# One graph-network kernel: the edge sums in 35 chunks a step and 45 half-width products instead of 36 chunks and 36 full-width products

## The reference

```python
xn = _layernorm(x)
msgs = edge_val[:, None] * xn[edge_src]                      # 212500 rows of 256
agg = jax.ops.segment_sum(msgs, edge_dst, num_segments=N)    # edge_dst is sorted
support = (1.0 + eps) * xn + agg
h = jax.nn.relu(support @ W1.T + b1)
x = x + (h @ W2.T + b2) + _L0_mix_ref(xn[None], ...)[0]
x = x + _L0_ffn_ref(_layernorm(x)[None], ...)[0]             # top-k routing, gelu, two products
```

## Time and profile before

| what | value |
|---|---|
| median of 3 runs | 2581.78 us |
| the profiled execution's own time | 2585.47 us |
| its span, first to last instruction | 2583.9 us |
| mean granted TensorE clock | 0.986 |
| TensorE busy | 2472.5 us, 96% |
| TensorE weight loads busy | 2151.3 us, 83% |
| GpSimd busy | 1712.5 us, 66% |
| VectorE busy | 1794.8 us, 69% |
| ScalarE busy | 1430.8 us, 55% |

### The profile page before, as it was taken

One profiled execution on the slowest core, in us unless ns is written; L12 is line 12 of the kernel. 1 busy time (PEld: TensorE's weight loads), 2 busy tenths in 40 slices (PEclk: granted clock), 3 DMA queues, 4 the chain that ended last, 5 costly groups with the idle time before them and its releaser, 6 DMA issues.

```text
span 2583.9 us, 41907 instructions
## 1 busy us (share of the span) xinstructions
PE 2472.5 (96%) x12655; PEld 2151.3 (83%) x12655; DVE 1794.8 (69%) x5939; ACT 1430.8 (55%) x3219; POOL 1712.5 (66%) x1881
## 2 busy tenths in 40 slices
PE   4789999999999999999999999999999999999996
PEld 4777888888888888888888888888888888888786
DVE  8847776776767768677677676776867767767567
ACT  3545665656656556466565664655646656556431
POOL 1247777777777777777777777777777777777400
PEclk9889999999999999999999999999999999999998
DMA  6734444344443444443434444344444343443338
GB/s 206 256 110 123 121 122 127 115 118 127 119 130 112 119 119 118 128 121 117 121 114 119 127 118 130 112 118 120 118 126 123 115 125 113 118 127 118 89 118 283
DMA packets 192003, 333.42 MB, mean 129 GB/s; under 512 B 46286, under 2 KB 133964, under 8 KB 191672
## 3 DMA queue, kind: packets, MB, share of 16 engines
q0 software_dynamic: 86752, 238.17, 31.6%
q1 hardware_dynamic: 105018, 92.42, 11.2%
HBM read 291.99 MB, written 38.46 MB: 128 GB/s over the span
## 4 chain that ended last, share of the span: by engine, by line
PE 86%; DVE 8%; DMA 3%; ACT 2%; issue 1%; SPq 0%; DVEq 0%
PE bank L1170 26%; PE qkv L1265 13%; PE bank L1277 13%; PE bank L1184 10%; PE bank L1214 6%; PE qkv L1194 5%; PE bank L1239 3%; PE bank L1230 3%; PE qkv L1193 2%; PE bank L1204 2%; DMA work<-in_x 2%; DVE rings L975 1%; DMA xn_dram<-work 1%; DVE work L422 1%; DVE work L393 1%; PE bank L1251 1%
## 5 line engine op out<-in xcount | busy, mean ns | idle before, releaser
L781 POOL DMA_INDIRECT rings<-xn_dram,window x1764 | 1686.7, 956 | 643.7 <-issue 377.2
L1170 PE MATMUL bank<-rings 128*128 128x256 f32 x3528 | 884.6, 380 | 16.1 <-DVE rings L975 13.2
L1170 PEld LDWEIGHTS bank<-rings 128*128 128x128 f32 x3528 | 653.8, 190 | 105.3 <-DVE rings L975 22.1
L975 DVE TENSOR_SCALAR rings<-iota,window_dst,window 128x128 f32<-128x128 f32 x1764 | 560.1, 358 | 160.8 <-PE bank L1170 138.8
L1265 PE MATMUL qkv<-work,ffn_weights 128*128 128x256 f32 x1568 | 365.5, 381 | 0.0
L1277 PE MATMUL bank<-ffn_weights,work 128*128 128x256 f32 x1568 | 362.0, 379 | 0.0
L871 ACT ACTIVATE work<-qkv,fb 128x256 f32<-128x256 f32 x392 | 160.1, 473 | 312.5 <-PE qkv L1265 312.0
L1277 PEld LDWEIGHTS bank<-ffn_weights,work 128*128 128x128 f32 x1568 | 297.2, 190 | 40.0
L1265 PEld LDWEIGHTS qkv<-work,ffn_weights 128*128 128x128 f32 x1568 | 295.7, 191 | 38.6
L1184 PE MATMUL bank<-resident,weights 128*128 128x256 f32 x1176 | 280.5, 382 | 0.0
L853 ACT ACTIVATE work<-bank 128x512 f32<-128x512 f32 x49 | 29.3, 597 | 403.2 <-PE bank L1222 403.2
(11 more groups left out here) (241 smaller groups left out, 3241.6 us busy)
## 6 DMA issues: line engine op xcount, KB each, us to landing
rings<-xn_dram,window POOLq DMA_INDIRECT x1764, 2.8
xn_dram<-work SPq DMA_DIRECT2D x14, 896.0 KB, 8.3
work<-xn_dram SPq DMA_DIRECT2D x49, 256.0 KB, 2.8
work<-in_x SPq DMA_DIRECT2D x48, 256.0 KB
out<-work SPq DMA_DIRECT2D x48, 256.0 KB
work<-in_x SPq DMA_DIRECT2D x7, 896.0 KB, 7.7
rings<-in_x SPq DMA_DIRECT2D x6, 896.0 KB, 9.4
rings<-out SPq DMA_DIRECT2D x6, 896.0 KB, 8.4
```

Source lines behind the costliest of these rows:

```text
L781: nc.gpsimd.indirect_dma_start(out=msg[q][:, :], out_offset=None, in_=xn_dram[:, :], in_offset=bass.IndirectOffsetOnAxis(ap=window[t % WIN ...
L975: v.tensor_scalar(sel[k % SEL_RING], iota[:, :], window_dst[b][:, k % SLOTS:k % SLOTS + 1], window[b][:, k % SLOTS, 2:3].bitcast(F32), ALU ...
L1170: te.matmul(agg[h], sel[k % SEL_RING], msg[q], start=first, stop=last, skip_group_check=True).then_inc(slot_used, 1)
```

## The change

The two accumulators of 128 nodes become four of 64: `agg[h][side * 64:(side + 1) * 64]`. A selection matrix has 64 columns, and a product writes 64 partitions of the accumulator, from partition 0 (side 0) or 64 (side 1). A step takes 35 chunks from the exact first edge of the *step*. Quarter q of the step's 256 nodes is multiplied with the chunks QUARTERS[q], which overlap at the borders: 10 + 12 + 12 + 11 = 45 products. Each chunk is gathered once; ten of them are used by two quarters. `products()` orders them so that sides alternate. If a quarter's edges lie outside its chunks, extra chunks are taken, whose number `tables_extra` works out on VectorE from the bounds (for any input; a second DMA of `dst` shifted by one edge tests whether `dst` is sorted).

Other edits: SEL_RING 12 to 22 (of half size), LEAD 8 to 12, two windows of a whole step instead of four of a tile, loaded in seven DMAs (one per block of chunks), `remainder` once a step, the orders PE_AT and DVE_AT, fewer end-of-row semaphores in the last stage, one reduction less and one compare and reduction more (`tables_order`) in the first part. GpSimd's second gather now stands behind a wait for `extra_stored` and two register loads.

```diff
-SEL_RING = 12
-LEAD = 8
+SEL_RING = 22
+LEAD = 12
 EARLY_EDGES = 12
-WINDOWS = 4
+WINDOWS = 2
+SLOTS = 35
+BLOCKS = (0, 7, 10, 15, 19, 24, 27, 35)
+QUARTERS = ((0, 10), (7, 19), (15, 27), (24, 35))
+LEFT = ((0, 1, 2, 3, 4, 5, 6, 7, 8, 9), (15, 16, 17, 18, 19, 20, 21, 22, 23, 24, 25, 26))
+RIGHT = ((10, 11, 12, 13, 14, 7, 8, 9, 15, 16, 17, 18), (27, 28, 29, 30, 31, 32, 33, 34, 24, 25, 26))
...
+def products():
+    order = []
+    for h in range(2):
+        for left, right in itertools.zip_longest(LEFT[h], RIGHT[h]):
+            order += [(2 * h + side, k) for side, k in enumerate((left, right)) if k is not None]
+    return order
...
         def tables_rows(pool):
+            pool.dma_start(rows_next[:, :, :].bitcast(I32), dst[1:ROWS + 1].rearrange("(c p j) -> p c j", p=P, j=P)
+                           ).then_inc(next_landed, 16)
...
+        def tables_order(dve):
+            v = nc.vector
+            dve.wait_ge(next_landed, 16)
+            v.tensor_tensor(rows, rows, rows_next.bitcast(I32), ALU.is_gt).then_inc(order_compared, 1)
+            dve.wait_ge(order_compared, 1)
+            v.tensor_reduce(unsorted_col, rows.rearrange("p c j -> p (c j)"), AX_X, ALU.max).then_inc(order_ready, 1)
...
+            tables_extra(dve)
...
-        PE_AT = dict(sup=0, x3=0, qkv=10, w1=1, h1=(12, 17, 20), w2=4, outT=(13, 23), ft=(16, 27), hid=(23, 23,
-                     27, 29), y=(31, 32, 32, 35))
+        PE_AT = dict(w1=5, w2=11, qkv=18, outT=22, ft=26, h1=30, late=34, hid=38, y=41)
...
+            for i in range(NS):
+                pool.wait_ge(window_landed[i % WINDOWS], WINDOW_DONE * (i // WINDOWS + 1))
+                for n, k in enumerate(GATHERS):
...
+                        pool.wait_ge(slot_used, RING + back * STEP_PRODUCTS + FREED[m] + 1)
...
+                    if n == 0:
+                        if i == 0:
+                            pool.wait_ge(extra_stored, 16)
+                        more = [pool.value_load(extra_count[0:1, 2 * i + h:2 * i + h + 1], min_val=0, max_val=ET)
+                                for h in range(2)]
...
+                v.tensor_scalar(sel[at_ % SEL_RING], iota[:, q * H:(q + 1) * H], window_dst[b][:, k:k + 1],
+                                window[b][:, k, 2:3].bitcast(F32), ALU.is_equal, ALU.mult).then_inc(sel_ready, 1)
...
-                te.matmul(agg[h], sel[k % SEL_RING], msg[q], start=first, stop=last,
-                          skip_group_check=True).then_inc(slot_used, 1)
+                te.matmul(agg[h][side * H:(side + 1) * H], sel[(i * STEP_PRODUCTS + n) % SEL_RING], msg[gathered % RING],
+                          start=first, stop=n == STEP_PRODUCTS - 1, skip_group_check=True).then_inc(slot_used, 1)
...
+                edges_to(PE_AT["w1"])
+                if j >= 0:
+                    tail_w1(j)
+                edges_to(PE_AT["w2"])
```

More of the change, by code:

```diff
@@ new lines, in rem_chunk @@
+                g.indirect_dma_start(out=rem_msg[:, :], out_offset=None, in_=xn_dram[:, :],
+                                     in_offset=bass.IndirectOffsetOnAxis(ap=rem_edges[:, 0:1], axis=0)
+                                     ).then_inc(rem_landed, 16)
+                for side in range(2):
+                    g.tensor_scalar(inside[:, side:side + 1], chunk, float(QUARTERS[2 * h + side][0]), BIG,
+                                    ALU.is_ge, ALU.mult)
+                g.tensor_scalar(dst_col, rem_edges[:, 1:2], float(-2 * P * i), None, ALU.add).then_inc(rem_dst_ready, 1)
@@ L1068, in step @@
                 last = i == NS - 1
[L1069 removed]
+                for k in range(STEP_PRODUCTS):
+                    if k == DVE_AT["stage"] and not last:
+                        start_step(i + 1)
                     ahead = k + LEAD
[L1071 removed]
+                    nxt = ahead >= STEP_PRODUCTS
                     if not (last and nxt) and not (i == 0 and ahead < EARLY_EDGES):
[L1073 to L1077 removed]
+                        edge(i + nxt, ahead % STEP_PRODUCTS)
                     if j >= 0:
@@ new lines, in step @@
+                if j >= 0:
+                    tail_w2(j, ran(i))
+                edges_to(PE_AT["qkv"])
+                mix_qkv(i, 1)
+                if i < NS - 1:
+                    mix_h1(i + 1, 0)
+                edges_to(PE_AT["outT"])
+                mix_outT(i, j, 0)
+                edges_to(PE_AT["ft"])
+                mix_ft(i, j, 0)
+                if i < NS - 1:
+                    mix_h1(i + 1, 1)
+                edges_to(PE_AT["h1"])
+                if i < NS - 1:
+                    mix_h1(i + 1, 2)
@@ new lines, in step @@
+                edges_to(PE_AT["late"])
+                mix_outT(i, j, 1)
+                if m is not None:
+                    ffn_hidden(m, 0, i)
+                    ffn_hidden(m, 1, i)
+                edges_to(PE_AT["hid"])
+                mix_ft(i, j, 1)
+                if m is not None:
+                    ffn_hidden(m, 2, i)
+                edges_to(PE_AT["y"])
+                if m is not None:
+                    ffn_hidden(m, 3, i)
+                    ffn_project(m, 0, i)
+                    ffn_project(m, 1, i)
```

421 lines of the change are left out of this document (256 added, 165 removed).

## The result

The change makes the kernel slower: 2657.8 us (median of 4 runs, 2657.5 to 2658.7) against 2581.4 us (4 runs of the kernel before, 2578.4 to 2582.5). The ratio is 1.030, 95% interval 1.028 to 1.032. The forecast was 2506 us, faster, and the time lies outside its range.

What follows compares the result with a forecast made beforehand. TensorE, 96% busy, was taken as the bound, with GpSimd's gathers close behind. From 2585.47 us, 85 saved over 49 steps (1.73 each) and 9 added ahead of the loop gave 2509.5, 2506 as a median; range 2455 to 2610.

Steps and rivals of the forecast that it cites:

- The edge products: On TensorE, half-width records on opposite halves overlap; a run of n takes (n + 1) x 0.216 us, 3.67 less a step.
- first part: Step up to `mix_outT(i,1)`: 8.86 us of products, 14.14 other work, 1.12 for width changes; 24.12 for 24.51, 0.39 saved.
- The rival of serial halves: TensorE's 90 half-width edge records run one after another at 0.216 us, 3.89 us a step more, 2782 us; chance 0.14.
- The rival of an array emptied at each change: Each change of width on TensorE costs 0.164 us (2572 us), or 0.354 with a weight load (2758 us); chance 0.20.
- The chains between the runs: ScalarE and VectorE's chain to the second `om` limits TensorE's saving: 23.96 us after; both parts save 2.07 us a step.
- The 0.43 us that the early `tail_supT` was to save: Putting `tail_supT` first in the step shortens the chain over ScalarE and VectorE by 0.43 us, to 23.96.
- VectorE writes 45 selections for 36: On VectorE, at most 3.2 us more selection work a step, in the 30% of the step in which it idles.
- the last 0.03: Chance 0.03 for a chain of waits made by the new orders, slower than forecast.
- The second part: Step after the first part: 11 products in three runs, 3.02 plus 0.48 us, for 5.18 before; 1.68 us saved.
- The gathers: GpSimd's 35 gathers at 1.25 us are 43.75 us a step, 393.8 in nine; rival that they take over, chance 0.13.
- the 3 us of waits in nine steps: Given back for gather waits as slack shrinks: nine steps take 404.4 us instead of 401.4, saving 1.73 us a step.
- The first part of the program: Ahead of the loop: 1.9 us VectorE pass, 2 us second dst load, 5.5 us later gathers; 9.4 us more in all.

Runs made afterwards that it cites:

- best version: Changed kernel with lead 16, `tail_w1` after 2 and `tail_w2` after 5 products, `tables_extra` behind the batch norm; 2534.9 us, 0.981 of the kernel before.
- experiment 4: Changed kernel with each half step's products ordered all of one side first, then the other, instead of alternating; 2887.9 us, 1.117 of the kernel before.
- Experiment 3: Changed kernel with `tail_w1` after 2 and `tail_w2` after 5 edge products instead of 5 and 11; 2624.5 us, 1.015 of the kernel before.
- experiment 1: Changed kernel with VectorE writing each selection 16 products ahead instead of 12; 2565.9 us, 0.993 of the kernel before.
- experiment 5: Changed kernel with the counting of extra chunks in `tables_extra` replaced by two memsets to zero; 2654.2 us, 1.027 of the kernel before.
- experiment 7: Changed kernel with lead 16 and `tables_extra` after the batch norm, counts read after step 0's last gather; 2564.3 us, 0.993 of the kernel before.
- Experiment 9: Kernel before with a lead of 10 selections instead of 8, ring of 12 unchanged; 2660.7 us, 1.031 of the kernel before.

## Why the prediction was wrong

**The edge products: the overlap right, the sum right by two errors.** They overlap, as forecast. In the best version TensorE waits in its first part only for `om`, 0.36 us, so 24.74 - 0.36 = 24.38 is an upper bound for its own time. The seven runs there, of 2, 3, 13 and four times 4 products, take 0.58, 1.12, 3.17, 1.45, 1.02, 1.13 and 1.08 us, together 9.55; 14.83 are left for the rest. The sum had 8.86 for such seven runs and 14.14 + 1.12 = 15.26 for the rest. So the runs cost 0.69 more: an odd product costs a whole pair where the sum gave it half, a run has 0.15 us on top, and in one run of four the last two products stand on the same side, which takes 1.45 us (368.43 to 369.88) and not 1.03. The rest costs 0.43 less. That the two nearly cancel, and 24.38 comes near the forecast 24.12, is luck.

The rival of serial halves is gone (experiment 4). The rival of an array emptied at each change is gone in its price: it had 25.30 for a first part of which TensorE itself needs at most 24.38. As a mechanism it isn't excluded. Its 0.164 a change stood on (n + 1) records a run; on two pairs of products, 0.86 us, two such changes make 1.19 for a run of four, and 1.13 was measured: 1.03 in the run, and 0.10 by which a neighbour of eight full-width records between two runs (1.93, 371.18 to 373.11) is longer than one with a run on one side (1.83, 384.68 to 386.51 in the best version). What is excluded is a weight load on top (0.354 a change, 1.57 for the run).

The Trainium skill, "TensorEngine Tiling (Array Packing)", Key Properties, has "Mode switching requires drain". The rows agree that a change costs something, with 1.13 us for a run of four whose two pairs of products take 0.86: 0.27 for its two changes together. They don't show that it is a drain.

**The chains between the runs: here it failed.** The prediction put the chain over ScalarE and VectorE at 23.96 us, that is 24.39 as measured before, less 0.43 for the transposes put first. It held everything else on it constant. Three terms of this were wrong:

- `tail_w2` has eleven products ahead of it instead of five. Eleven in two runs take 2.88 us, five took 2.16: 0.72 us later, where the chain had nothing.
- The 0.43 us that the early `tail_supT` was to save are not on this chain. `combine` waits for `tail_w2` (L1397, 3.01 us), and the edge product that moved behind the transposes still stands ahead of `tail_w2`. The two together are 1.15 of the 1.18 us by which `combine` is late: after 7.80 us where 6.62 was implied. Experiment 3 gives 1.19 of it back at that point, and 0.7 in the step.
- "VectorE writes 45 selections for 36 [...] in the 30% of the step in which it idles", so they stood in the sum at nothing. Their durations are indeed nothing (0.9 us a step). But I counted how many and how long, not where they stand. With a lead of 12, product 31 (from 0) has its selection at position 19, behind the second `om` (position 18), and product 33 behind `tail_rstd` (position 20), and products 0 to 33 now stand ahead of `mix_outT(i,1)`. Before, a lead of 8 sufficed: the last of the 24 products ahead of the turn had its selection at the start of position 15, ahead of the `om` that stands there. That is the stretch of 1.95 us for 0.12, and experiment 1 takes it away.

The forecast for the first part, 24.12, was measured at 27.23. Of the 3.11 us between them the late `combine` is 1.18 and the selections that stand behind `om` are 1.79 (1.95 less the 0.16 that the forecast's 24.12 leaves behind its chain of 23.96); the other 0.14 lie in the stretch between. The whole loop bears this out: the rows of L1351 have 63.5 us more where 83 fewer were forecast, 146.5 us in 48 intervals, 3.05 each. The two parts of the step give 3.11 + 0.16, less the 0.34 that the forecast had given back for the gathers, 2.93. Nine steps take 431.7 us (L1380, 365.41 to 797.13) for the 404.4 forecast. None of the three was among the rivals; the last 0.03 was given to "a chain of waits made by the new orders", without a mechanism or a price. The orders that the prediction shows are those of TensorE and GpSimd, and it is VectorE's that decided.

**The second part: right.** 1.68 us fewer were forecast; 23.19 less 21.67 (48.9 - 27.23) is 1.52.

**The gathers: not reached.** No step of any version came under 46.4 us with a feed-forward part, so the floor of 43.75 was not tested, and the 3 us of waits in nine steps can't be judged. The best version takes 409.9 us for nine steps (354.88 to 764.82) against 393.8 of gathers, and its edge products wait 2.8 us for gathers in the whole program.

**The first part of the program: right.** 9.8 us for 9.4, and by its terms: 4.1 for 3.9 ahead of the first gather, 5.7 for 5.5 behind it (experiment 5). Only the signs were set down wrong. "Near 155" for the batch norm and "near 158.5" for the second gather leave out the prediction's own 3.9 us; with them they are 158.9 and 162.4, and 160.07 and 163.32 were measured. VectorE's timeline:

```profile
146.24 0.17 DVE L529 SCALAR_TENSOR_TENSOR work<-work 128x7 f32<-128x7 f32 x1 [0.52 <-ACT work L564]
148.66 0.06 DVE L366 MEMSET work<- 1x1 f32 x1 [2.25 <-PE bank L609]
...
160.07 0.14 DVE L649 TENSOR_SCALAR work<-bank 128x1 f32<-128x1 f32 x1
```

The normalization is 4.1 us later (142.14 before). From there `tables_extra` waits another 2.25 us for TensorE, for the last use of a bank, which I had missed, and takes 11.4, a little less than the 9.4 plus 2.4 to 4.8 of the prediction. The batch norm comes 13.83 us behind L529 (146.24 to 160.07) instead of the 8.75 before, 5.1 more, where 4.5 were forecast; in experiment 7 it is 8.75 again (146.54 to 155.29). The second gather comes 7.57 us behind the first instead of the 1.33 before, 6.2 more for 5.5.

## What to carry to other kernels

When a change moves work on the engine that bounds, go through the queue of every engine that feeds it, and ask of each item that is needed ahead of a point where its producer puts it: an item of 0.3 us that stands behind a chain of 17 us comes when the chain has ended, however idle the producer is on average. A lead is bounded from below by the blocks that the items stand behind and from above by the ring less the products not yet read; both ends cost some 3% here (a lead of 12 for 16 in a ring of 22: 3.6%; one of 10 for 8 in a ring of 12: 3.1%). And a move is worth only what the longer of two chains allows: the same four products were worth 52 us moved in one version and cost 37 in another.

## What the runs showed of the hardware

Edge products of 64 columns on opposite halves go through TensorE in pairs, at 0.43 us a pair, with 0.15 us a run on top: two products take 0.58 us (355.85 to 356.43 in the best version), four 1.03, five and six both 1.44 (369.74 to 371.18 is the run of six), seven 1.87, thirteen 3.17. An odd product costs a whole pair; the forecast's (n + 1) records of 0.216 had it at half. A run of four whose last two products stand on the same side takes 1.45, as three pairs do. On the same side each product takes the 0.43 that a pair takes (3.16 = 7 x 0.43 + 0.15), so the halves give a factor of 1.69 in a run of seven and 1.60 in one of five. The Trainium skill, "TensorE: Matmul & The Clock Gate", Part 3, states 2.38 for three column tiles; no run here has three.

The Trainium skill, "Perfetto Trace Analysis", Tensor Engine Instruction (MATMUL, LD_WEIGHTS), says that VectorE works strictly in the order of its queue. Experiment 9 shows what that means: 499 us of VectorE's waits in front of selections, none of which the work behind them needed.
